# Layer 0 of a three-layer graph network: neighbour rows split in a rounded part and a rest for one 260-column matmul per tile, and row statistics taken over two interleaved blocks

## The reference, cut to what matters

```python
def sage(h, w_self, w_neigh, b):
    agg = jax.ops.segment_sum(h[src], dst, num_segments=n) * inv_deg
    return h @ w_self + agg @ w_neigh + b
h = jnp.maximum(_layernorm(x, axis=-1), 0.0)      # 100000 x 128
h = jax.nn.relu(sage(h, ws0, wn0, b0))            # 128 -> 256
h = jax.nn.relu(sage(h, ws1, wn1, b1))            # 256 -> 256
h = sage(h, ws2, wn2, b2)                         # 256 -> 128
return x + h
```

## Time and profile before

| | us |
|---|---|
| median of the timed runs | 4343.96 |
| their lowest and highest (3 runs) | 4340.45, 4346.31 |
| the profiled execution, first to last instruction (span) | 3894.5 |
| median less span | 449.5 |
| layer 0, first to last `cat_lo` | 85.7 to 2112.1 |

### The profile page before, as it was taken

The page is one execution under the profiler, slowest core; times in us unless marked ns, Lnnn a source line. Parts: engine busy times, 40 slices in busy tenths (PEclk is TensorE's granted clock), DMA queues, the critical chain, the costliest instruction groups (busy, mean ns, idle before and its releaser), DMA issues. The chain is left out here.

```text
span 3894.5 us, 112772 instructions
## 1 busy us (share of the span) xinstructions
PE 3532.1 (91%) x22513; PEld 3153.3 (81%) x22513; DVE 3468.6 (89%) x12047; ACT 3041.3 (78%) x8036; POOL 2555.3 (66%) x3691
## 2 busy tenths in 40 slices
PE   1999999999999999999998999999999987677676
PEld 1888888888888888888887888988988876566665
DVE  7999999999999999999997888888888877777777
ACT  4888877788888888878886777887887777777777
POOL 2655655566566665655564777777777767777776
PEclk9999999999999999999999999999999995655666
DMA  2444444444444444444444888888888879999998
GB/s 69 130 140 141 141 140 129 137 140 141 140 141 141 141 141 141 141 136 140 140 142 138 233 244 247 244 245 245 245 246 243 242 221 262 264 263 266 264 263 247
DMA packets 1040320, 727.59 MB, mean 187 GB/s; under 512 B 102725, under 2 KB 1012173, under 8 KB 1040125
## 3 DMA queue, kind: packets, MB, share of 16 engines
q1 hardware_dynamic: 854277, 569.67, 47.6%
q0 software_dynamic: 80336, 104.91, 10.5%
q10 hardware_dynamic: 105600, 51.92, 4.5%
HBM read 451.32 MB, written 360.71 MB: 209 GB/s over the span
## 5 line engine op out<-in xcount | busy, mean ns | idle before, releaser
L613 POOL DMA_INDIRECT loaded_rows<-in_x,gather_at x784 | 922.6, 1177 | 389.0 <-issue 254.7
L1445 PE MATMUL ps_out<-w_hi,hid_hi 128*128 128x512 f32 (+1 forms) x3136 | 1139.3, 363 | 40.9 <-DVE layer_mem L1336 34.1
L1445 PE MATMUL ps_out<-w_hi,hid_lo 128*128 128x512 f32 (+1 forms) x3136 | 1055.6, 337 | 0.0
L1445 PE MATMUL ps_out<-w_lo,hid_hi 128*128 128x512 f32 (+1 forms) x3136 | 1054.6, 336 | 0.0
L649 POOL DMA_INDIRECT layer_mem<-p_rows,gather_at x784 | 803.3, 1025 | 265.5 <-issue 189.8
L1445 PEld LDWEIGHTS ps_out<-w_hi,hid_hi 128*128 128x128 f32 x3136 | 589.7, 188 | 165.9 <-issue 55.0
L1445 PEld LDWEIGHTS ps_out<-w_hi,hid_lo 128*128 128x128 f32 x3136 | 589.1, 188 | 71.7
L662 POOL DMA_INDIRECT layer_mem<-z_rows,gather_at x528 | 525.9, 996 | 180.4 <-issue 138.4
L1445 PEld LDWEIGHTS ps_out<-w_lo,hid_hi 128*128 128x128 f32 x3136 | 591.0, 188 | 58.5
L1445 PE MATMUL ps_hid<-cat_hi,w_hi 128*128 128x256 f32 x1568 | 447.1, 285 | 11.0 <-DVE cat_lo L1251 10.0
L839 ACT ACTIVATE layer_mem<-iota_row,triple_node 128x128 f32<-128x128 f32 x1056 | 337.3, 390 | 151.8 <-issue 54.3
(11 more groups left out here) (173 smaller groups left out, 9079.1 us busy)
## 6 DMA issues: line engine op xcount, KB each, us to landing
p_rows<-stored_rows SPq DMA_DIRECT2D x392, 256.0 KB, 2.5
q_rows<-layer_mem SPq DMA_DIRECT2D x392, 256.0 KB, 2.8
loaded_rows<-q_rows SPq DMA_DIRECT2D x392, 256.0 KB
loaded_rows<-y_rows SPq DMA_DIRECT2D x264, 192.0 KB
layer_mem<-in_x SPq DMA_DIRECT2D x264, 192.0 KB
out_rows<-stored_rows ACTq DMA_DIRECT2D x264, 192.0 KB
loaded_rows<-in_x SPq DMA_DIRECT2D x392, 128.0 KB, 2.1
z_rows<-layer_mem SPq DMA_DIRECT2D x392, 128.0 KB
```

The costliest lines, as they stand in the source:

```text
L613: pool.indirect_dma_start(raw[s.slot][0:rows, 2 + j, :], None, table, bass.IndirectOffsetOnAxis(gather_at[s.slot][0:rows, j:j + 1], axis=0 ...
L1445: ins = nc.tensor.matmul(o, a, b, start=n == 0, stop=n == len(terms) - 1)
```

## The change

- Statistics: two `bn_stats` instead of four. Each reads two blocks of 128 with their elements alternating (element 0 of block A, element 0 of block B, element 1 of A, ...). The instruction keeps statistics of even and odd elements apart, so its six outputs are the count, mean and sum of squares of each block. The four `bn_aggr` go; `std` takes the sum of squares with the scale 1/128, and the mean is read from `stats`.
- Neighbour rows: ACT normalises them before the own rows and then copies them, rounded, into `halves` (a new instruction of 2x130 elements). DVE subtracts to get the rest, into the same tile beside the rounded part (new, 2x130 elements, `nbr_split`).
- Sums: for each tile one FP32R matmul of 260 columns, the rounded sums and the sums of the rest side by side in one bank, instead of one fp32 matmul of 130 columns. `ps_agg` gets two banks and `ps_hid` gives one up.
- DVE adds own rows and the rounded sums as before, and then, after waiting for that result, adds the sums of the rest (new, 2x128 elements, `rest_added`).
- PE now waits for `nbr_split` instead of `normed` before the sums, ACT waits for `rest_added` before the mean, and `ps_hid` waits for the ReLU of the preceding pair, not the one before it.
- Layer 1's `nbr_hi` and `nbr_lo` become views of `halves`.

The core of the diff:

```diff
-                    for j in range(4):
-                        last = dve.bn_stats(stats[t.half][:, j, :], raw[t.slot][:, j, :])
+                    if t.has(2):
+                        dve.wait_ge(L0.shift_ready, t.back(2).n + 1)
+                    for k in range(2):
+                        last = dve.bn_stats(stats[t.half][:, k, :],
+                                            raw[t.slot][:, 2 * k:2 * k + 2, :].rearrange("p j f -> p f j"))
                     last.then_inc(L0.stats_done, 1)
+                v = first.back(2)
+                if v.live():
+
+                    dve.wait_ge(L0.nbr_hi_ready, v.n + 1)
+                    if v.has(2):
+                        dve.wait_ge(L0.summed, v.back(2).n + 1)
+                    dve.tensor_tensor(halves[v.half][:, :, 1, :], h_nbr[v.half][:, :, :],
+                                      halves[v.half][:, :, 0, :].bitcast(FP32), ALU.subtract).then_inc(L0.nbr_split, 1)
...
-                    for j in range(4):
-                        last = dve.bn_aggr(moments[t.half][:, j, :], stats[t.half][:, j, :])
-                    last.then_inc(L0.moments_ready, 1)
...
                     dve.reciprocal(inv_degree[:, two], degree[s.half][:, :]).then_inc(L0.recip_done, 1)
+                    dve.wait_ge(L0.own_added, s.n + 1)
+                    dve.tensor_tensor(agg[s.half][:, :, 0:D], agg[s.half][:, :, 0:D], lo_sums[:, :, 0:D], ALU.add
+                                      ).then_inc(L0.rest_added, 1)
...
+                        act.wait_ge(L0.nbr_normed, t.n + 1)
+                        if t.has(2):
+                            act.wait_ge(L0.summed, t.back(2).n + 1)
+                        act.activation(halves[t.half][:, :, 0, :], h_nbr[t.half][:, :, :], ACT.Copy
+                                       ).then_inc(L0.nbr_hi_ready, 1)
...
-                    if t.has(2):
-                        pe.wait_ge(L0.h1_made, t.back(2).n + 1)
+                    if t.has(1):
+                        pe.wait_ge(L0.h1_made, t.back(1).n + 1)
...
-                    pe.wait_ge(L0.normed, t.n + 1)
+                    pe.wait_ge(L0.nbr_split, t.n + 1)
                     if t.has(1):
...
-                        pe.wait_ge(L0.own_added, t.back(1).n + 1)
+                        pe.wait_ge(L0.rest_added, t.back(1).n + 1)
...
                     for j in range(2):
-                        last = nc.tensor.matmul(ps_agg[:, j * H:j * H + D + 2], select[t.half][:, j, :].bitcast(FP32),
-                                                h_nbr[t.half][:, j, :], start=True, stop=True)
+                        last = nc.tensor.matmul(agg_bank[j], select[t.half][:, j, :],
+                                                halves[t.half][:, j, :, :].rearrange("p t f -> p (t f)"),
+                                                start=True, stop=True)
```

More of the change, by code:

```diff
@@ L213, in build @@
         raw = [t[:, :].rearrange("p (j f) -> p j f", j=4) for t in loaded_rows]
-        stats = [sb(f"stats{i}", [P, 4, 6]) for i in range(2)]
-        moments = [sb(f"moments{i}", [P, 4, 2]) for i in range(2)]
+        stats = [sb(f"stats{i}", [P, 2, 6]) for i in range(2)]
+        moments = [t[:, :, :].rearrange("p k (e t) -> p (k e) t", e=2) for t in stats]
+        MEAN, SQUARES = 1, 2
         std = [sb(f"std{i}", [P, 4]) for i in range(2)]
@@ L225, in build @@
         nbr = [part(2, H) for i in range(SLOTS)]
-        nbr_hi = [sb(f"nbr_hi{i}", [P, L1_SPLIT, H], FP32R) for i in range(2)]
-        nbr_lo = [sb(f"nbr_lo{i}", [P, L1_SPLIT, H], FP32R) for i in range(2)]
         gather_at = [sb(f"gather_at{i}", [P, SHARED], I32) for i in range(SLOTS)]
+        halves = [sb(f"halves{i}", [P, 2, 2, D + 2], FP32R) for i in range(2)]
         select = [sb(f"select{i}", [P, 2, P], FP32R) for i in range(2)]
+        nbr_hi, nbr_lo = ([t[:, :, :, :].rearrange("p j t f -> p (j t f)")[:, at:at + H].rearrange("p (j f) -> p j f", j=1)
+                           for t in halves] for at in (0, H))
         degree = [sb(f"degree{i}", [P, 2]) for i in range(2)]
@@ L297, in build @@
         b2_held = ps_out[1][:, 0:D]
-        strips = [ps_agg[:, D + 2 + j * H:D + 2 + j * H + TP] for j in range(2)]
+        strips = [ps_agg[:, j * 512 + 2 * (D + 2):j * 512 + 2 * (D + 2) + TP] for j in range(2)]
         w_loaded, bias_loaded = sem("w_loaded"), sem("bias_loaded")
@@ L742, in step @@
                     if t.live():
-                        act.wait_ge(L0.moments_ready, t.n + 1)
-                        act.activation(std[t.half][:, :], moments[t.half][:, :, 1], ACT.Sqrt, bias=eps_col[:, :]
+                        act.wait_ge(L0.stats_done, t.n + 1)
+                        act.activation(std[t.half][:, :], moments[t.half][:, :, SQUARES], ACT.Sqrt, bias=eps_col[:, :],
+                                       scale=1.0 / D
                                        ).then_inc(L0.std_ready, 1)
@@ L751, in step @@
                         for m in range(2):
-                            last = act.activation(h1[t.half][:, m, :], ps_hid[t.half][:, m * PAIR:(m + 1) * PAIR],
+                            last = act.activation(h1[t.half][:, m, :], ps_hid[:, m * PAIR:(m + 1) * PAIR],
                                                   ACT.Relu, bias=b0_col[:, m:m + 1])
@@ L773, in step @@
                         if t.has(2):
-                            act.wait_ge(L0.summed, t.back(2).n + 1)
+                            act.wait_ge(L0.nbr_split, t.back(2).n + 1)
                             act.wait_ge(L0.turned, t.back(2).n + 1)
-                        for j in range(4):
-                            rows = h_own[t.half][:, j, :] if j < 2 else h_nbr[t.half][:, j - 2, 0:D]
-                            if general and j >= 2:
+                        for j in range(2, 4):
+                            rows = h_nbr[t.half][:, j - 2, 0:D]
+                            if general:
                                 last = act.activation(rows, raw[t.slot][:, j, :], ACT.Copy)
@@ L782, in step @@
                                                       bias=shift[t.half][:, j:j + 1], scale=rstd[t.half][:, j:j + 1])
+                        last.then_inc(L0.nbr_normed, 1)
+                        for j in range(2):
+                            last = act.activation(h_own[t.half][:, j, :], raw[t.slot][:, j, :], ACT.Relu,
+                                                  bias=shift[t.half][:, j:j + 1], scale=rstd[t.half][:, j:j + 1])
                         last.then_inc(L0.normed, 1)
+                        act.wait_ge(L0.nbr_normed, t.n + 1)
[3 more added lines that the diff above has]
+                                       ).then_inc(L0.nbr_hi_ready, 1)
                 return step
@@ L1078, in general @@
                         dve.wait_ge(ge_turned, i + (first + 1))
-                        mine(dve.tensor_scalar(ge_same[:, :], ps_hid[1][0:EP, 0:EP], ge_dst[:, :], None,
+                        mine(dve.tensor_scalar(ge_same[:, :], ps_hid[0:EP, 0:EP], ge_dst[:, :], None,
                                                op0=ALU.is_equal))
```

37 lines of the change are left out of this document (18 added, 19 removed).

## The result

The changed kernel took 4427.78 us, median of 4 runs (4426.09 to 4430.42), beside 4344.37 of the kernel before on the same chip (4 runs, 4340.45 to 4346.31): a ratio of 1.0196, 95% interval 1.0181 to 1.0210, **83 us slower**. The forecast was 4408, 64 us slower, with 4377 to 4493 as its own range.

What follows compares the result with a forecast made beforehand. PE and DVE were taken as almost balanced, with DVE bounding after the change: first eight chunks 5.39 against 5.19 us a step, +71 us, last chunk -7, together +64, 4408 us; range 4375 to 4570, the forecast's own 4377 to 4493.

Steps and rivals of the forecast that it cites:

- Who is the bound: Layer 0, first eight chunks: DVE's own time rises to 5.27 us a step, above PE at 4.90, and sets the pace.
- the near balance before: Layer 0, first eight chunks before the change: DVE's own time 4.98 us a step against 5.10 of PE.
- DVE's own step: Layer 0, DVE from one bn_stats to the next without a round: 4.59 us before, 4.88 after, net +0.29.
- the +0.04: DVE's second addition in layer 0 must wait for the first one's result: 0.04 us a step.
- The waits that I kept: First eight chunks: 28 us of data and issue waits stay, 0.08 us a step, beside 0.04 for the tables.
- The alternating read: New bn_stats jumping 512 bytes each element: taken to cost nothing; the rival of a slow read, +156 us, 4564, had 20%.
- The write row: Nearest profile row for the alternating read: a write to every fourth word, 1.11 against 0.70 us for 528 elements.
- the last chunk: Layer 0's last 44 steps, without rounds: DVE 4.88, PE 4.90, with friction 4.95 us against 5.10, so -7 us.
- rival 2: ACT's rounding copy comes late by 0.2 us in about 260 steps without a round: +52 us on top, 4460; chance 13%.
- 0.2 until ACT sees it: Handoff from PE's hidden product (1.47 us) to ACT's ReLU, a term in the copy's timing: 0.2 us.
- my chain for the copy: From cat_lo's end to rounded rows ready on ACT: 5.35 us, against DVE's need at 5.44, fitting by 0.1.
- The sums are not free of the subtraction: PE's sums wait for DVE's subtraction, which ends 1.0 us into DVE's step, during the 1.47 us hidden product: free.

Runs made afterwards that it cites:

- e4: Changed kernel without DVE's second addition and the wait in it (sums of the rest computed, not added): 4405.26 us, ratio 1.0040 to the kernel before.
- e6: Changed kernel without the subtraction and the second addition, so neighbour sums are of rounded rows only: 4313.72 us, ratio 0.9827 to the kernel before.
- e9: Changed kernel, unedited, profiled on a chip where the kernel before takes 4391.61 us: 4467.78 us, ratio 1.0171 to the kernel before.
- e3: Changed kernel with bn_stats reading its 256 elements in order, not alternating (statistics mix two rows): 3963.19 us, ratio 1.0182 to the kernel before.
- e0: Kernel before, no edit, profiled again as baseline on the fastest chip: 3897.71 us, span 3895.9.
- e1: Kernel before with the new statistics alone (two bn_stats, no bn_aggr, no split): 3839.79 us, ratio 0.9861 to the kernel before.
- e5: Changed kernel with ACT's rounding copy moved between the two own rows, 0.39 us earlier: 4446.32 us, ratio 1.0130 to the kernel before.
- e2: Changed kernel with the old statistics (four bn_stats, four bn_aggr behind select): 4197.62 us, ratio 1.0777 to the kernel before.

## Why the prediction was right, and where it was not

**Who is the bound.** Right. DVE takes over, PE waits for `cat_lo` ahead of the hidden product, 115.2 us in 275 times up to 2050 us, 0.3 a step where 0.4 was forecast. Both halves of the argument were needed, the addition on DVE and the near balance before. `e4` and `e6` show it from the other side: each instruction taken off DVE makes the kernel faster, with PE's work as it is.

**DVE's own step.** 4.96 for 4.88. The pair of `bn_stats` is 0.68 for 0.65; `stored_rows` costs 0.60 instead of 0.575, in all kernels where it stands behind `select` rather than behind `bn_aggr`; the dependent second addition makes `inv_degree` and its wait 0.10 to 0.12 for 0.075, as the +0.04 said; the rest is 0.01 here and there. The subtraction (0.33) and the addition (0.34) were priced right. The rows show no dearer read out of PSUM. The Trainium skill (VectorE: DVE Perf Modes, "The TRN2 errata"), with 120 cycles fixed out of PSUM and 58 out of SBUF, would by an estimate have put the addition 0.06 above the subtraction. The trace doesn't agree: 0.34 against 0.33.

**The waits that I kept.** 28 us for data and issue were carried over from the earlier trace rows. In `e9`, where DVE is the bound, `bn_stats` waits 1.2 us for data and 0.7 for issue. A DVE that is late for everything doesn't wait for a gather. The 0.08 us a step that I kept for them were nearly all too much, and DVE's own step was 0.08 longer than forecast. By luck the two cancel: `e3` on chip A has early steps of 5.39, just the forecast, against 5.20 of `e0`, which is +67 us where +71 were forecast (and 0.20 x 347 is 69, not 71; my sum was 2 us too high). Its span is 3961.1 where 3958 were forecast. The number was better than its parts. Two things go with it. After itself was never run on A, only `e3`, whose `bn_stats` are 0.02 us a step shorter. And on the chips where after was run it lost 83, 78 and 76 us, against the 64 of the forecast.

**The alternating read.** Taken at nothing, and it is 0.01 us an instruction, 0.02 a step. The write row was a poor stand-in for it. The Trainium skill's rule (Vector Engine (DVE) Microarchitecture Reference, "Measured stream behaviour on trn2") of a port that slows down when a stream jumps every element isn't what this instruction shows, with 421 ns against 412; the exception in the same section, a one-source instruction that alternated between two regions at full rate, is.

**The step that failed: the last chunk, and with it rival 2.** I had PE bound at 5.10 there, and both engines at 4.90 after: -7 us. It came out at -2 on A (5.04 in `e3` for 5.09) and at +5 on D. On A the terms of DVE make it: its own step is 4.94 there and not 4.88, two of the 40 steps also build tables and take 6.1 us, 0.06 on the mean, its waits add another 0.06, and the last two steps, where the pipeline runs empty, give 0.03 back. DVE bounds this chunk too, and a PE at 4.90 or less had nothing to say in it. (That PE's own step before was 5.02 and not 5.10, by `e1`, changes nothing in this sum, since before did take 5.09.) On D, "0.2 until ACT sees it" was too short besides. Here is the last matmul of a hidden product and ACT's ReLU that waits for it, in `e3` on chip A and in `e9` on chip D:

```profile
2047.25 0.28 PE L1467 MATMUL ps_hid<-cat_hi,w_lo 128*128 128x256 f32 x1
```
```profile
2047.67 0.84 ACT L757 ACTIVATE layer_mem<-ps_hid,b_col 128x256 f32<-128x256 f32 x2 [0.67 <-PE ps_hid L1467]
```
```profile
2050.46 0.28 PE L1467 MATMUL ps_hid<-cat_hi,w_lo 128*128 128x256 f32 x1
```
```profile
2051.20 0.84 ACT L757 ACTIVATE layer_mem<-ps_hid,b_col 128x256 f32<-128x256 f32 x2 [1.05 <-PE ps_hid L1467]
```

That is 0.42 and 0.74 from start to start. Over all such waits between 1900 and 2060 us the median is 0.32 on A (21 of `e3`) and 0.75 on D (20 of `e9`, from 0.32 to 0.86). Put into my chain for the copy in place of 0.12 + 0.2, that is the same on A and 0.43 more on D, where there was 0.1 us of room. And there the distance from `bn_stats` to the subtraction shows it: in the early steps 0.66 to 0.67 in the mean on A (its minimum is 0.65), but 0.76 on D, where most are 0.68; in the last chunk 0.85. That is 0.08 x 347 + 0.17 x 44, about 35 us of late copies on D; on C, where they are alike, `e5` gets 21 back by moving the copy. So rival 2 holds in part on the slower chips, and hardly at all on A. It was priced at +52 us on steps without a round, and weighed against the forecast as if only one of the two could be; they came together.

Which side the delay is on can be read from the semaphore events of the traces. ACT isn't slow: it starts 0.02 us after the semaphore of the hidden product is set, in `e3` and in `e9`. It is the semaphore that comes late. From 150 to 1850 us it is set 0.29 to 0.30 us after the start of the last matmul in every step of `e3`; in `e9` after 0.70 in the median, and up to 1.29. Semaphores that ACT and DVE set are as prompt on D as on A (for most, 0.01 us after the end of the instruction).

The kernel before is slower in layer 0 on D as well (early 5.29 against 5.20 on A). There too PE's semaphores come late, 0.61 us after the start of the last matmul of the sums in the median, against 0.29 on A, and DVE waits 28.5 us for the sums against 7.7. This hides most of the 35 us in the difference: +77 on D between before and after, +66 on A between before and `e3`.

Two small slips in the prediction's sums moved nothing: the chain for the copy adds up to 5.34 and not 5.35, and the upper end for DVE is +0.42 and not +0.43.

**The sums are not free of the subtraction.** I said that it would be done while PE is still in the hidden product. With PE waiting for `cat_lo`, and DVE's subtraction waiting for the copy, the two come near each other: 22.4 us of waits in 33 times name the subtraction, and 95.6 more stand there as issue. PE has slack now, so I take it that this costs nothing by itself, but no run shows that alone. It shows how a wait that "fits" depends on who is late.

**What stays open.** Why PE's semaphores come late on some chips: instruction lengths and matmul spacing are the same there. From the start of the last matmul to ACT's start, the median in `e4` was 1.02 on C, so it is no fixed delay. Also open is why PE's matmuls follow each other 1.5% faster with the new statistics. That the split would gain if its two DVE instructions ran on an idle engine wasn't tried; POOL has most idle time, but the rows here give no price for such work on it.

## What to carry to other kernels

When two engines are nearly in balance, price a trade between them by net time per step on the engine that gets the work: here 0.20 us off PE was bought with 0.67 on DVE, and only the 0.39 saved by the other half of the change (0.10 on `bn_stats`, 0.29 on `bn_aggr`) and the ring it opened kept the loss at 2%. Test the halves of such a change apart; the half that only removed work was the whole gain, 1.4%, and the two together lost it. Follow each ring of waits round once and add it up, with the handoffs between engines as terms of their own: a ring of 5.60 us looks like slack on both engines (`e2`), and a busy PE is not yet a PE at its own pace.

## What the runs showed of the hardware that was not expected

- The same kernel takes 3897 us on one chip and 4344 to 4392 on others; a stretch of layers 1 and 2 moves 244 to 245 GB/s on chips like A and 190 on D. A span and a median from two chips can't be subtracted.
- From the start of the last matmul to the start of the ACT instruction that waits for it: 0.32 us in the median on chip A, 0.75 on D. ACT starts 0.02 us after the semaphore on both; the semaphore itself is set 0.30 us after the start of that matmul on A and 0.70 on D.
- A `bn_stats` over two rows in alternation runs within 9 ns of one in order (421 and 412 ns for 256 elements).
- Back-to-back matmuls of 512 columns are 0.230 us apart in the median in `e1` and 0.233 before, with the same granted clock of 1.00 (2.4 GHz).
